# Another order of the pieces on four engines in a two-layer graph network kernel

## The reference

```
layer 0:  x = x + adj @ (h @ W0) + bias0
layer 1:  f = h @ fc_w + fc_b                     (8 heads of 256)
          q, k = f @ q_w + q_b, f @ k_w + k_b     (per head and node)
          a = softmax(leaky_relu(q + k^T + (1 - adj) * -1e9))
          x = x + sigmoid((a @ f) @ fp_w + fp_b + h)
```

## Time and profile before

| | us |
|---|---|
| median of 3 runs | 1577.28 (1573.38, 1577.28, 1577.47) |
| the profiled execution, its own time | 1573.69 |
| its span, first to last instruction | 1571.9 |
| PE busy in the span | 1526.9 (97%) |
| DVE busy | 1336.9 (85%) |
| ACT busy | 1203.5 (77%) |
| POOL busy | 938.4 (60%) |
| DMA engines' mean share (queue 1) | 10.1% |

### The profile page before, as it was taken

How to read it: one execution, slowest core, us unless ns; L and a number is a source line. 1 busy time by engine, 2 the same in 40 slices (tenths; PEclk the granted TensorE clock), 3 DMA queues, 4 the chain that set the end, 5 groups by cost and what they waited for, 6 DMA issues and landing times.

```text
span 1571.9 us, 32998 instructions
## 1 busy us (share of the span) xinstructions
PE 1526.9 (97%) x9920; PEld 1352.5 (86%) x9920; DVE 1336.9 (85%) x4719; ACT 1203.5 (77%) x3667; POOL 938.4 (60%) x1244
## 2 busy tenths in 40 slices
PE   4599999999999999999999999999999999999998
PEld 4588888888888888888888888888888888888887
DVE  1388898898898889889889889988988988988986
ACT  1277887887788788788788778878878878877875
POOL 1356656666665665665666666566566566666653
PEclk9799999999999999999999999999999999999999
DMA  4000110110110110011011011011001101101100
GB/s 163 14 31 25 41 40 20 40 40 20 40 40 21 39 40 32 28 40 40 20 40 40 20 40 40 22 38 40 33 27 40 40 20 40 40 20 40 40 12 16
DMA packets 20324, 55.90 MB, mean 36 GB/s; under 512 B 2896, under 2 KB 3280, under 8 KB 19920
## 3 DMA queue, kind: packets, MB, share of 16 engines
q1 hardware_dynamic: 20304, 55.67, 10.1%
HBM read 38.88 MB, written 16.78 MB: 35 GB/s over the span
## 4 chain that ended last, share of the span: by engine, by line
PE 96%; DVE 1%; issue 1%; POOL 1%; DMA 1%; SPq 1%; ACT 0%; POOLq 0%; DVEq 0%; ACTq 0%
PE gbank L222 45%; PE ybank L222 23%; PE front L222 9%; PE gbank L323 7%; PE sbank L316 4%; PE front L276 3%; PE front L292 2%; PE gbank L238 1%; PE front L277 1%; DMA kqb<-q_b_dram 1%; SPq L192 1%; PE front L243 0%; DVE att L499 0%; PE front L246 0%; DVE att L506 0%
## 5 line engine op out<-in xcount | busy, mean ns | idle before, releaser
L789 POOL TENSOR_TENSOR att<-att,rinv 128x512 f32<-128x512 f32 x256 | 266.8, 1042 | 351.8 <-DVE rinv L511 351.8
L644 ACT ACTIVATE att<-att 128x128 f32<-128x128 f32 x1024 | 396.8, 392 | 65.0 <-DVE att L506 64.9
L222 PE MATMUL gbank<-m_hi,hT_lo 128*128 128x512 f32 x1024 | 414.3, 405 | 0.4 <-DVE g_lo L479 0.4
L222 PE MATMUL gbank<-m_lo,hT_hi 128*128 128x512 f32 x1024 | 406.9, 397 | 0.0
L222 PE MATMUL gbank<-m_hi,hT_hi 128*128 128x512 f32 x1024 | 405.4, 396 | 0.0
L637 ACT ACTIVATE g_hi<-gbank 128x512 fp32r<-128x512 f32 x512 | 287.0, 586 | 100.9 <-PE gbank L222 100.8
L479 DVE TENSOR_TENSOR g_lo<-gbank,g_hi 128x512 fp32r<-128x512 f32 x512 | 348.7, 681 | 15.1 <-ACT g_hi L637 15.1
L222 PE MATMUL ybank<-g_hi,pT_lo 128*128 128x256 f32 x1024 | 299.4, 292 | 0.0
L222 PE MATMUL ybank<-g_lo,pT_hi 128*128 128x256 f32 x1024 | 289.2, 282 | 0.0
L222 PE MATMUL ybank<-g_hi,pT_hi 128*128 128x256 f32 x1024 | 288.6, 282 | 0.0
L499 DVE CUSTOM_DVE_ANT_0 att<-sbank,t_pos 128x128 f32<-128x128 f32 x1024 | 235.9, 287 | 14.4 <-issue 14.4
(11 more groups left out here) (94 smaller groups left out, 3078.6 us busy)
## 6 DMA issues: line engine op xcount, KB each, us to landing
g_in<-graph_dram SPq DMA_DIRECT2D x64, 512.0 KB, 3.4
out_dram<-late SPq DMA_DIRECT2D x64, 256.0 KB, 2.0
late<-fc_wT_dram SPq DMA_DIRECT2D x2, 1024.0 KB, 6.0
fp_sb<-fp_w_dram SPq DMA_DIRECT2D x1, 2048.0 KB, 11.2
hmask<-head_mask_dram SPq DMA_DIRECT2D x1, 512.0 KB, 10.3
w_f<-w_dram SPq DMA_DIRECT2D x1, 256.0 KB, 10.2
b_row<-bias_dram SPq DMA_DIRECT2D x1, 128.0 KB, 10.6
c_row<-fp_b_dram SPq DMA_DIRECT2D x1, 128.0 KB, 12.1
```

The source lines that it names most:

```text
L222: mm = pe.matmul(out_ap, w, m, start=first and n == 0, stop=last and n == len(terms) - 1)
L644: e = act.activation(a[:, s], a[:, s], ACT.Exp, scale=-1.0, bias=a[:, CH + h:CH + h + 1], accum_out=esum[j][c][:, h:h + 1])
L789: gp.tensor_tensor(a, a, rinv[j][c][:].unsqueeze(2).broadcast_to([P, HC, P]), ALU.mult)\
```

## The change

The pieces, their operands and all buffers stay. RING and G_RANK have another order, and so have the calls in step on PE, DVE, ACT and POOL; the order on SP stays. Relative to the scores of pair i, several pieces now stand in another step: on PE, transpose_h, queries_keys and project 0 of pair i+1 are in step i, and aggregate of pair i+2, so PE's pipeline starts two steps ahead where it was one, and ACT's three where it was two. In the diff below, twelve leading blanks are left out of every line of the steps.

```diff
--- before.py
+++ after.py
@@ -26,10 +26,10 @@
 KQ = 32
 
 
-RING = ((("t", 3), -1), (("g", 2), 0), (("g", 0), 0), (("g", 1), 0), (("g", 4), 0), (("t", 0), 0),
-        (("g", 5), 0), (("g", 3), 0), (("g", 7), 0), (("t", 1), 0), (("g", 6), 0), (("t", 2), 0))
+RING = ((("g", 1), 0), (("g", 3), 0), (("g", 2), 0), (("t", 0), 0), (("g", 6), 0), (("g", 4), 0),
+        (("g", 5), 0), (("t", 2), 0), (("t", 1), 0), (("g", 7), 0), (("g", 0), 1), (("t", 3), 0))
 SRING = ((0, 0), (1, 0), (2, 0), (3, 0))
-G_RANK = (0, 1, 0, 1, 0, 1, 1, 0)
+G_RANK = (0, 1, 1, 0, 0, 1, 0, 1)
 
 
 def gnn_pair(nc, graph, identity, head_mask, row_coef, w0, bias0, fc_wT, fc_b, qk_w, q_b, k_b, fp_w, fp_b, out):
@@ -337,44 +337,48 @@
 
 def step(i, q):
     if has(i):
-        transpose_h(i, q)
-    if has(i - 1):
-        attend(i - 1, 0, 1)
-        transpose_p(i - 1, 1, 1)
-    if has(i):
-        h_ready(i)
-        queries_keys(i, q)
-        project(i, q, 2)
-        project(i, q, 0)
         scores_ready(i)
         scores(i, q, 0, 0)
+    if has(i - 1):
+        attend(i - 1, 0, 1)
+    if has(i):
+        scores(i, q, 0, 1)
         project(i, q, 1)
-        scores(i, q, 0, 1)
     if has(i - 1):
         attend(i - 1, 1, 0)
-    if has(i + 1):
-        aggregate(i + 1, 1 - q)
     if has(i):
         scores(i, q, 1, 0)
     if has(i - 1):
         attend(i - 1, 1, 1)
     if has(i):
+        project(i, q, 3)
+        scores(i, q, 1, 1)
+        project(i, q, 2)
+        transpose_p(i, 0, 0)
+    if has(i + 1):
+        transform(i + 1, 1 - q)
+    if has(i):
+        project(i, q, 6)
         project(i, q, 4)
-        scores(i, q, 1, 1)
-        transpose_p(i, 0, 0)
         project(i, q, 5)
-    if has(i + 1):
-        transform(i + 1, 1 - q)
-    if has(i):
-        project(i, q, 3)
+        transpose_p(i, 1, 0)
+        attend(i, 0, 0)
+    if has(i + 1):
+        transpose_h(i + 1, 1 - q)
+    if has(i):
+        transpose_p(i, 0, 1)
         project(i, q, 7)
-        transpose_p(i, 0, 1)
-        attend(i, 0, 0)
-        project(i, q, 6)
-        transpose_p(i, 1, 0)
+    if has(i + 1):
+        h_ready(i + 1)
+        queries_keys(i + 1, 1 - q)
+        project(i + 1, 1 - q, 0)
+    if has(i):
+        transpose_p(i, 1, 1)
+    if has(i + 2):
+        aggregate(i + 2, q)
 
 setup()
-pipeline(pe, step, 1, 1)
+pipeline(pe, step, 1, 2)
 
         @block.vector
         def _(dve):
@@ -518,20 +522,27 @@
     dve.tensor_tensor(y[:], ybank_jd[:], feats_c[q], ALU.add).then_inc(v_y, 1)
 
 def step(i, q):
-    if has(i - 1):
-        pT_low(i - 1, 1, 1)
+    if has(i):
+        kq_high(i)
+        kq_parts(i)
+        spread(i, q)
+    if has(i - 1):
+        g_low(i - 1, 7)
     if has(i):
         mask_ready(i)
         mask_min(i, q, 0, 0)
-        g_low(i, 2)
+    if has(i - 1):
+        pT_low(i - 1, 1, 1)
+    if has(i):
         leaky(i, 0, 0)
         mask_min(i, q, 0, 1)
-        g_low(i, 0)
+    if has(i + 1):
+        ah_rest(i + 1, 1 - q)
+    if has(i):
         leaky(i, 0, 1)
         inverse(i, 0, 0)
         mask_min(i, q, 1, 0)
-    if has(i + 1):
-        ah_rest(i + 1, 1 - q)
+        g_low(i, 0)
     if has(i - 1):
         add_feats(i - 1, 1 - q)
     if has(i):
@@ -539,9 +550,9 @@
         mask_min(i, q, 1, 1)
         leaky(i, 1, 0)
         leaky(i, 1, 1)
-        g_low(i, 4)
+        g_low(i, 3)
         inverse(i, 0, 1)
-        pT_low(i, 0, 0)
+        g_low(i, 2)
     if has(i + 1):
         residual0(i + 1, 1 - q)
     if has(i):
@@ -550,25 +561,22 @@
         stats1(i + 1, 1 - q)
         mean1(i + 1, 1 - q)
     if has(i):
-        g_low(i, 5)
+        pT_low(i, 0, 0)
         inverse(i, 1, 1)
-        g_low(i, 3)
-        pT_low(i, 0, 1)
-        g_low(i, 7)
+        g_low(i, 6)
     if has(i + 3):
         stats0(i + 3, 1 - q)
-    if has(i + 1):
-        hT_low(i + 1, 1 - q)
-    if has(i):
-        g_low(i, 6)
-        pT_low(i, 1, 0)
-    if has(i + 1):
-        kq_high(i + 1)
+    if has(i):
+        g_low(i, 4)
     if has(i + 3):
         mean0(i + 3, 1 - q)
-    if has(i + 1):
-        kq_parts(i + 1)
-        spread(i + 1, 1 - q)
+    if has(i):
+        g_low(i, 5)
+    if has(i + 1):
+        hT_low(i + 1, 1 - q)
+    if has(i):
+        pT_low(i, 1, 0)
+        pT_low(i, 0, 1)
 
 setup()
 pipeline(dve, step, 1, 3)
@@ -663,48 +671,51 @@
     act.activation(sg[:], th[:], ACT.Copy, scale=0.5, bias=0.5).then_inc(a_sg, 1)
 
 def step(i, q):
-    if has(i - 1):
-        pT_high(i - 1, 0, 1)
-        g_high(i - 1, 7)
-    if has(i):
-        h1_relu(i, q)
-        hT_high(i, q)
-    if has(i - 1):
-        g_high(i - 1, 6)
-        pT_high(i - 1, 1, 0)
-    if has(i + 1):
-        h0_relu(i + 1, 1 - q)
-    if has(i - 1):
-        pT_high(i - 1, 1, 1)
-    if has(i):
-        queries(i, q)
-    if has(i + 1):
-        h0_high(i + 1, 1 - q)
+    if has(i):
+        g_high(i, 1)
+        exp(i, 0, 1)
+    if has(i - 1):
+        tanh(i - 1)
+    if has(i):
+        g_high(i, 3)
+    if has(i - 1):
+        sigmoid(i - 1)
+    if has(i):
+        g_high(i, 2)
+        exp(i, 1, 0)
+        pT_high(i, 0, 0)
+        exp(i, 1, 1)
+        g_high(i, 6)
+        g_high(i, 4)
+    if has(i + 1):
+        h1_relu(i + 1, 1 - q)
+    if has(i):
+        g_high(i, 5)
+    if has(i + 1):
+        hT_high(i + 1, 1 - q)
+    if has(i):
+        pT_high(i, 1, 0)
+        pT_high(i, 0, 1)
+        g_high(i, 7)
+    if has(i + 3):
+        aT_high(i + 3, 1 - q)
+    if has(i + 1):
+        queries(i + 1, 1 - q)
+    if has(i):
+        pT_high(i, 1, 1)
     if has(i + 2):
-        aT_high(i + 2, q)
-    if has(i):
-        g_high(i, 2)
-        g_high(i, 1)
-        g_high(i, 0)
-        exp(i, 0, 0)
-    if has(i + 1):
-        ah_small(i + 1)
-        ah_high(i + 1, 1 - q)
-    if has(i):
-        exp(i, 0, 1)
-    if has(i - 1):
-        tanh(i - 1)
-        sigmoid(i - 1)
-    if has(i):
-        g_high(i, 4)
-        pT_high(i, 0, 0)
-        exp(i, 1, 0)
-        exp(i, 1, 1)
-        g_high(i, 5)
-        g_high(i, 3)
+        ah_small(i + 2)
+        ah_high(i + 2, q)
+    if has(i + 3):
+        h0_relu(i + 3, 1 - q)
+    if has(i + 1):
+        exp(i + 1, 0, 0)
+        g_high(i + 1, 0)
+    if has(i + 3):
+        h0_high(i + 3, 1 - q)
 
 setup()
-pipeline(act, step, 1, 2)
+pipeline(act, step, 1, 3)
 
         @block.gpsimd
         def _(gp):
@@ -803,10 +814,21 @@
     gp.tensor_tensor(res[q], sg[:], x1[q], ALU.add).then_inc(g_res, 1)
 
 def step(i, q):
+    if has(i):
+        h0_low(i, q)
+    if has(i - 2):
+        feats(i - 2, q)
     if has(i + 1):
         minus_mean0(i + 1, 1 - q)
-    if has(i):
+        rstd0(i + 1, 1 - q)
+        shift0(i + 1, 1 - q)
+    if has(i):
+        inputs(i, q)
         ah_low(i, q)
+    if has(i - 1):
+        normalise(i - 1, 0, 0)
+    if has(i + 1):
+        aT_low(i + 1, 1 - q)
     if has(i - 2):
         residual1(i - 2, q)
     if has(i - 1):
@@ -817,22 +839,10 @@
         minus_mean1(i, q)
         rstd1(i, q)
         shift1(i, q)
-    if has(i + 1):
-        rstd0(i + 1, 1 - q)
     if has(i - 1):
         normalise(i - 1, 1, 1)
-    if has(i + 1):
-        shift0(i + 1, 1 - q)
-    if has(i - 1):
-        feats(i - 1, 1 - q)
-    if has(i + 1):
-        inputs(i + 1, 1 - q)
-        h0_low(i + 1, 1 - q)
     if has(i + 2):
-        aT_low(i + 2, q)
         variance0(i + 2, q)
-    if has(i):
-        normalise(i, 0, 0)
 
 setup()
 gp.wait_ge(v_set, SETUP_V)
```

More of the change, by code:

```diff
@@ L339, in step @@
                 if has(i):
-                    transpose_h(i, q)
+                    scores_ready(i)
+                    scores(i, q, 0, 0)
                 if has(i - 1):
                     attend(i - 1, 0, 1)
-                    transpose_p(i - 1, 1, 1)
                 if has(i):
-                    h_ready(i)
-                    queries_keys(i, q)
-                    project(i, q, 2)
-                    project(i, q, 0)
-                    scores_ready(i)
-                    scores(i, q, 0, 0)
+                    scores(i, q, 0, 1)
                     project(i, q, 1)
-                    scores(i, q, 0, 1)
                 if has(i - 1):
                     attend(i - 1, 1, 0)
-                if has(i + 1):
-                    aggregate(i + 1, 1 - q)
                 if has(i):
@@ L361, in step @@
                 if has(i):
-                    project(i, q, 4)
+                    project(i, q, 3)
                     scores(i, q, 1, 1)
+                    project(i, q, 2)
                     transpose_p(i, 0, 0)
-                    project(i, q, 5)
                 if has(i + 1):
@@ L368, in step @@
                 if has(i):
-                    project(i, q, 3)
-                    project(i, q, 7)
-                    transpose_p(i, 0, 1)
-                    attend(i, 0, 0)
-                    project(i, q, 6)
-                    transpose_p(i, 1, 0)
+                    project(i, q, 6)
+                    project(i, q, 4)
+                    project(i, q, 5)
```

(39 more changed lines are left out.)

1 line of the change is left out of this document (removed).

## The result

The kernel after takes 1599.3 us in the median (1597.1 to 1600.7) against 1575.5 for the kernel before on the same chips: ratio 1.0148, 95% interval 1.0134 to 1.0163, slower by some 23 us. The forecast was 1576, 23 us too low. The measured time lies in the stated range of 1571 to 1605 only because the range took in the rivals; the first rival's 1595 to 1602 holds it. The profiled execution has a span of 1598.0 us, against 1571.9.

What follows compares the result with a forecast made beforehand. PE, full in the steady part, was the bound: period unchanged, seams 0, fill -0.6 and +0.8, drain -0.4, sum -0.2, so 1573.5 against the profiled 1573.7; set between that and the median 1577.3 at 1576, range 1571 to 1605.

Steps and rivals of the forecast that it cites:

- the first rival: residual1 gets the port between the two leaky; xb then holds spread, S00 0.30 to 0.42 late, 1595 to 1602; chance 0.3.
- PE as the bound, and 62 times the hole: Steady part: PE is always busy, the change can't shorten it, and a hole costs 62 times its length.
- The layout of the period: New 23.2 us period laid out from S00 of a pair: all waits met, spread starting at 21.32 with slack 0.5.
- V: Time in the period when mean0 is done and POOL's last group starts; forecast 16.4, xb at V + 3.74.
- The step that failed: At the leaky pair on DVE: second leaky keeps the port, residual1 follows, xb frees spread in time; no hole.
- second rival: t_pos gets the port ahead of spread; S00 up to 0.45 late, up to 28 us, 1580 to 1604; chance 0.1.
- The seams: Joins between different pieces on PE: 0 a period, range -0.05 to +0.08, or -3 to +5 us.
- third rival: Seams and fill come out better: -0.05 a period and 2 to 3 us less in the fill; 1569; chance 0.05.
- Fill and drain: Start and end of the run: fill -0.6 and +0.8, drain -0.4, sum -0.2 us.
- Loads: "10 us of cover": Load of pair i+3 on SP: issued near -0.5, takes 3.4, first read near 15; no cost, 10 us of cover.
- That leaky's hold costs nothing: Leaky pair on DVE, kernel before: one stands 1.05 us behind residual1, at no cost as DVE has 11% to spare.
- A two-SBUF-input op on DVE stands while a POOL op runs: Rule read from leaky's 1.05 us stand beside residual1, applied to spread beside POOL's ops.

Runs made afterwards that it cites:

- inputs early: Kernel after with inputs (xb, t_pos) moved right behind h0_low on POOL and feats behind shift0, nothing left out; 1572.6 us, ratio 0.9976 to the kernel before.
- Run 8: Kernel after with sigmoid ahead of g_high 3 on ScalarE; 1595.4 us, ratio 1.0122 to the kernel before.
- run 4: Kernel before, in its old order, with three sums into a scratch tile ahead of xb on POOL; 1603.3 us, ratio 1.0173.
- the repaired kernels: Kernels after with inputs early, with 256-column work added on POOL, or with leaky apart and load freed, also combined; 1571.6 to 1573.6 us.
- run 2: Kernel after with g_low 3 put between the two leaky on VectorE, nothing left out; 1587.0 us, ratio 1.0065 to the kernel before.
- runs 1: Kernel after with residual1 cut to 2 of its 512 columns, most of the output's last sum left out; 1571.5 us, ratio 0.9974 to the kernel before.
- run 3: The kernel called inputs early: kernel after with xb and t_pos right behind h0_low on POOL; 1572.6 us, ratio 0.9976 to the kernel before.
- run 7: Kernel after with an extra 64-column sum on POOL ahead of each h0_low; 1589.4 us, ratio 1.0081 to the kernel before.
- run 6: Kernel after with an extra 256-column sum on POOL ahead of each h0_low; 1572.8 us, ratio 0.9983 to the kernel before.

## Why the prediction was wrong

**PE as the bound, and 62 times the hole** held, in before and in every run with PE full.

**The layout of the period** held: 21.32 was laid out for spread's start, 21.28 measured (717.63, with S00 at 696.35 by the chain, 9.93 ahead of transform); for V the first rival had 17.2 to 17.3, measured 713.43, which is 17.08; xb 20.9 to 21.0, measured 21.07. In the pair shown two errors cancel in xb's start: V came 0.1 to 0.2 early, and from V to xb it is 3.99 where 3.74 was laid out, mostly because h0_low starts 0.32 behind variance0 and not 0.15. In the other kind of pair it is 741.01 - 737.23 = 3.78. The order of events at the leaky pair was right too, leaky first by 0.1.

**The step that failed** is "If the second leaky, queued right behind the first, keeps the port ... No hole. This I take." It doesn't keep it: residual1, waiting, got in between, pair after pair, and the first rival, at 0.3, was what happened: a hole of 0.42 a period in the mean where none was forecast. The reason given for keeping it, that DVE's ops overlap by 0.08 and the port may never look free, is refuted by the 2.40. POOL didn't come late to it either: residual1 went on at about 705.43 + 0.45 = 705.88, and the first leaky's 0.61 to 0.69 from 705.33 end at 705.94 to 706.02. Nothing in the trace of before showed a hand-over with both sides queued, and between the two I took the one that left the kernel as it was.

**The rival's size**: 0.30 to 0.42 a period. Against the same order free of holds (inputs early), whose S00 of pairs 1 and 63 stand here,

```profile
103.39 0.44 PE L316 MATMUL sbank<-rk,lq 128*128 128x512 f32 x1
...
1539.23 0.50 PE L316 MATMUL sbank<-rk,lq 128*128 128x512 f32 x1 [0.24 <-DVE rk L475]
```

(1539.23 - 103.39) / 62 = 23.16, it is 23.58 - 23.16 = 0.42, the upper end. That is a mean of two kinds of pairs, about 0.2 and 0.7, and neither lies within 0.30 to 0.42: that the mean does is in part luck. The prediction laid out one kind only. From spread's end to the matmul's start its sum has 0.03 to 0.06; the second kind shows 0.05 (741.46 + 1.92 to 743.43), the first 0.23 (719.79 to 720.02). Run 8 has both values too, turn about, and run 4 has 0.05 to 0.06 throughout; what adds the 0.2 isn't known. In the second rival's "up to 0.45" this term is left out; with it the bound is 0.50.

**The seams** were taken as 0 with a bound of -0.05. They are worth 23.16 - 23.22 = -0.06 a period, 1435.84 - 1439.51 = -3.7 us in all, just past the bound; PE is full in both kernels, so this is its own work, and it is why the repaired kernels beat the kernel before. Which seams give it wasn't taken apart. The third rival had the sign for the period, but not for the fill, and I gave it 0.05.

**Fill and drain** were put at -0.2. With inputs early they come to 103.39 + (1568.8 - 1539.23) = 132.96 against 105.35 + (1571.9 - 1544.86) = 132.39, +0.6: small, as forecast, but of the other sign. In the kernel after they come to 106.27 + 29.63 = 135.90, 2.9 more than with inputs early. No hold makes that: it is there before the first scores. The S00 of pair 0, in the kernel after and with inputs early:

```profile
85.12 0.44 PE L316 MATMUL sbank<-rk,lq 128*128 128x512 f32 x1
```

```profile
82.05 0.63 PE L316 MATMUL sbank<-rk,lq 128*128 128x512 f32 x1
```

They are 3.1 apart, and the two kernels differ in nothing but POOL's list. Set-up, which is the same in every kernel here, took longer: ScalarE's last m_hi starts at 47.8 in the kernel after and at 43.7 with inputs early, at 44.2 in the kernel before, and between 43.7 and 49.8 over all the profiled executions. So about 3 of the 26.1 us between the two spans say nothing of the order.

**Loads: "10 us of cover"** was wrong. I looked at the conditions of the load itself and not at the store that stands ahead of it on SP. In the kernel after the load is issued at 708.37 and lands near 711.8, and stats0 starts at 711.84: hardly any cover. It cost next to nothing there (2 waits, 1.0 us between 150 and 1500), but half of the repair in run 2.

**That leaky's hold costs nothing** in the kernel before held; in the new order it costs through what it delays (runs 1 and 3). "A two-SBUF-input op on DVE stands while a POOL op runs" was too wide: it is shown for residual1, xb and feats, POOL sums of two inputs with 512 columns. The small steps and t_pos ran on beside spread without holding it (run 3). So the second rival, which has t_pos hold spread for most of its 1.08, had its mechanism wrong.

## What to carry to other kernels

On a core whose TensorE is full, reordering can win little and lose much; lay out, beside the semaphores, every place where a VectorE op with two SBUF inputs meets a GpSimd op, and see which one starts first, and by how many tenths of a microsecond. Keep a POOL op like xb (two inputs, 512 columns, 1.3 us) from starting just ahead of such a DVE op whose result TensorE wants next; moving it behind, even by adding work, is enough. For a transfer, the cover is what is left after everything ahead of it on its queue.

## What the runs showed of the hardware

- The port between VectorE and GpSimd is handed to whoever waits, also between two queued ops of one engine, in both directions (pair of leaky 2.40 with residual1 1.74; xb, then spread 2.16, then t_pos 1.94). The Trainium skill ("SBUF — State Buffer", section "Who interferes with whom") says that issue order decides who blocks; run 7 agrees down to 0.06 us, for xb. That the waiting side comes between two queued ops it doesn't say.
- A GpSimd op on 128x2 is held like a large one, but doesn't hold like one: rstd0 stood for 1.06 us behind spread (1.77 for 0.71, run 3), while spread took 1.21 or 1.22 in the 32 pairs in which rstd0 was already running when it started. The small steps of a layernorm can lose time to VectorE, and in these runs they cost it at most some hundredths of a microsecond.
- t_pos (128x256, one tensor input, 1.08 us) is held too (1.94), but holds only at its start: with t_pos 0.07 us ahead a leaky stood for 0.19 (run 6), 0.20 ahead spread stood for 0.06, 0.28 ahead it didn't stand. By these numbers it lets go some 0.26 us from its start, where xb keeps the port to 0.12 before its recorded end. That the first has the port for its whole instruction, which the prediction took over, held for xb and residual1 and not for t_pos and rstd0. What makes the difference wasn't tested.
- A recorded length holds the standing time, and the held op goes on before the recorded end of the other: spread, 717.63 + 2.16 - 1.21 = 718.58, where xb's record ends at 718.70.
- In the kernel after and in run 7 xb's start against spread's alternates from pair to pair by about 0.3 us. Of the 0.26 in the kernel after, 0.17 lie between variance0 and h0_low (713.43 to 713.75 against 737.23 to 737.38). What makes the two kinds of pairs differ isn't known.
